# The edges of a fused two-layer decoder kernel: other orders for the first loads, the first rounds and the last ones

## The reference

```python
x = layernorm(x + L0_attn(x, Wq, Wk, Wv, Wo, lambdas, ln_w))   # differential attention, 16 heads of 2, 4 kv heads
x = layernorm(x + L0_xattn(x, k, fside, ctx, ctx, 8))          # a long convolution over the sequence, gated by ctx
x = layernorm(x + L0_ffn(x, gate_up, down, router_w))          # 8 experts, top 2, silu gate
x = layernorm(x + L1_attn(x, w_qkv, w_o))                      # causal attention, 16 heads of 32
x = layernorm(x + L1_xattn(x, mask, ctx, ctx, wq, wk, wv, wo)) # one head of 512: softmax((x wq)(ctx|x wk)^T) v, then wo
x = layernorm(x + L1_ffn(x, W_gate, W_qkv))                    # gate picks one head's k and v per token; attention with 16 query heads
return x

def L1_ffn(x, W_gate, W_qkv):
    gating = softmax(x @ W_gate.T); idx = argmax(gating)
    q, k, v = split(x @ W_qkv.T, 3)
    k_shared = k[head idx];  v_shared = v[head idx] * max(gating)
    return softmax(causal(q_h @ k_shared.T / sqrt(hd))) @ v_shared     # for every head h
```

## Time and profile before

| stretch of the span (us) | stage | PE busy (us) | PE idle (us) |
|---|---|---|---|
| 0 to 496 | front | 460.56 | 35.4 |
| 496 to 750 | long convolution | 252.92 | 1.1 |
| 750 to 880 | middle | 123.58 | 6.4 |
| 880 to 1199 | experts | 316.95 | 2.1 |
| 1199 to 1360 | tail: start, rounds 0 and 1 | 148.16 | 12.8 |
| 1360 to 2085 | tail: steady and first closing rounds | 715.07 | 9.9 |
| 2085 to 2162 | tail: closing rounds, last batch | 56.53 | 20.5 |

### The profile page before, as it was taken

The page is one execution under the profiler, slowest core; times in us unless marked ns, Lnnn a source line. Parts: engine busy times, 40 slices in busy tenths (PEclk is TensorE's granted clock), DMA queues, the critical chain, the costliest instruction groups (busy, mean ns, idle before and its releaser), DMA issues. The chain is left out here.

```text
span 2161.9 us, 29351 instructions
## 1 busy us (share of the span) xinstructions
PE 2073.8 (96%) x11935; PEld 1211.4 (56%) x11935; DVE 1191.6 (55%) x1827; ACT 515.7 (24%) x783; POOL 579.7 (27%) x542
## 2 busy tenths in 40 slices
PE   7899999989999999999999998999999999999996
PEld 5444444434444477565565655656666666666654
DVE  2566666667777754122222326366757575847466
ACT  1444444440000121110111122122222222222111
POOL 2122222227999600111110312112222212121112
PEclk9999999999999999999999999999999999999998
DMA  8950000105111046421121602101010101000000
GB/s 173 101 52 30 30 30 20 61 21 220 43 43 43 25 164 230 157 69 64 64 68 54 219 1 99 49 1 49 1 59 1 59 1 40 1 30 11 1 11 20
DMA packets 66178, 130.62 MB, mean 60 GB/s; under 512 B 6432, under 2 KB 19872, under 8 KB 66048
## 3 DMA queue, kind: packets, MB, share of 16 engines
q1 hardware_dynamic: 45392, 76.44, 13.8%
q10 hardware_dynamic: 14976, 33.69, 4.2%
q0 software_dynamic: 5680, 18.62, 2.9%
HBM read 97.40 MB, written 41.81 MB: 64 GB/s over the span
## 5 line engine op out<-in xcount | busy, mean ns | idle before, releaser
L1006 PE MATMUL conv_conv<-kv,toep 128*128 128x512 f32 x576 | 247.6, 592 | 0.1
L2578 DVE RECIPROCAL tail_inv<-tail_ring 128x256 f32<-128x256 f32 x60 | 105.4, 1756 | 178.2 <-PE tail_ring L1893 178.0
L1566 PE MATMUL moe_gu_ps<-gu,xT_tile 128*128 x608 | 192.4, 459 | 0.0
L1006 PEld LDWEIGHTS conv_conv<-kv,toep 128*128 128x128 f32 x576 | 109.4, 190 | 138.2 <-issue 129.6
L1040 POOL TENSOR_TENSOR kv<-vT,cT 128x512 f32<-128x512 f32 x128 | 147.2, 1175 | 16.6 <-PE conv_conv L1006 12.8
L2258 POOL TENSOR_TENSOR tail_rstd_x<-tail_rstd_x,const_minus_half 128x2 f32<-128x2 f32 x31 | 21.7, 701 | 477.0 <-DVE tail_rstd_x L2529 477.0
L1566 PEld LDWEIGHTS moe_gu_ps<-gu,xT_tile 128*128 128x128 f32 x608 | 112.3, 190 | 66.5 <-issue 17.8
L2266 POOL TENSOR_SCALAR_AFFINE_SELECT tail_expT<-tail_expT 128x1024 f32<-128x1024 f32 x63 | 70.0, 1112 | 245.2 <-ACT tail_expT L2350 244.7
L574 POOL TENSOR_SCALAR_AFFINE_SELECT front_expT<-front_expT 128x2048 f32<-128x2048 f32 x32 | 64.2, 2007 | 213.5 <-ACT front_expT L630 213.5
L1648 DVE TENSOR_TENSOR moe_hid<-moe_gu_ps,moe_silu 128x352 f32<-128x352 f32 x39 | 20.5, 524 | 171.1 <-PE moe_gu_ps L1566 171.1
L1547 POOL DMA_INDIRECT xg<-x_after,tokens x37 | 35.0, 946 | 282.0 <-PE moe_xT_ps L1561 254.9
(11 more groups left out here) (409 smaller groups left out, 4010.5 us busy)
## 6 DMA issues: line engine op xcount, KB each, us to landing
toep<-toeplitz SPq DMA_DIRECT2D x32, 320.0 KB, 2.9
y_slots<-moe_y ACTq DMA_DIRECT2D x39, 256.0 KB, 2.0
gu<-in_L_ffn_gate_up_proj SPq DMA_DIRECT2D x5, 1408.0 KB, 12.7
toeplitz<-filt_rows SPq DMA_DIRECT2D x1, 6144.0 KB, 66.9
front_e<-in_ctx SPq DMA_DIRECT2D x8, 512.0 KB, 5.7
toeplitz<-filt_rows SPq DMA_DIRECT2D x2, 2048.0 KB, 89.5
x_after<-x SPq DMA_DIRECT2D x8, 512.0 KB, 4.9
tail_x<-x_after SPq DMA_DIRECT2D x8, 512.0 KB, 3.7
```

The costliest lines, as they stand in the source:

```text
L1006: ins = pe.matmul(bank, toep[p][:, mat * P:(mat + 1) * P], kv[p][:, c].rearrange("p b j i -> p (b j i)"), start=n == 0, stop=n == len(PART ...
L1566: ins = pe.matmul(gu_ps[:, s % 2, h, 0:HID], (xT if s else mid.xT_first)[:, c, :], wgu[c][:, e, h * HID:(h + 1) * HID], start=c == 0, stop ...
L2578: link.after(dve.reciprocal(inv[c % 2][:], bank[:, S:2 * S]))
```

## The change

It moves instructions and drops one PSUM view; no product is added or removed. In the order of the program:

- Front, loads: SP issues x of batch 0, wv, wk, wq, then the filter and the rest; wq goes through SP's queue and no longer through ACT's. PE waits for wv and wk apart, and for the first constant alone before the first transposes. ACT regroups its half of wq before it drains the first values.
- Front, round 1 (a = 0): the first two `weigh` stand ahead of `scoreT` 2 and 4 (`soon`), as they already do for the last batch. The transposes of batch 3 move from the head of round 3 to behind `scoreT(1, 0)` of round 2.
- Front, last batch: DVE's `combine(7, 0, 1)` goes ahead of the second residual and the statistics of batch 6.
- Middle: PE's first pieces in another order.
- Tail start: the second half of the last `ctx_queries` goes behind the first `turn`, and the projections, scores and the second `turn` of batch 0 are interleaved anew.
- Tail round 1: `cross_turn(0, 1)` ahead of `weigh(P, 1, 1)` on PE; on DVE the norm of batch 2 and `mix(P, 1, 3)` earlier.
- Closing rounds: `maxima(A, h, 1)` ahead of `add_shared(a)`; `pick("v", c, 1)` behind `add_shared(h)`.
- Last batch: `ring_s` and the fourth exponential buffer go; of the four transposed score products only the second uses the ring's banks, the fourth comes after two `weigh`.

```diff
-        pe.wait_ge(constants_made, 7)
+        pe.wait_ge(constants_made, 1)
         for r, d, a, f, u in rounds():
-            if d is not None and d != 2: turn_input(d)
+            if d is not None and d not in (2, 3): turn_input(d)
             if d == 0:
+                pe.wait_ge(constants_made, 7)
                 xT_taken(d)
-                pe.wait_ge(weights_loaded, 32)
+                pe.wait_ge(weights_loaded["wv"], 16)
                 value(d)
+                pe.wait_ge(weights_loaded["wk"], 16)
                 key(d)
...
                 scoreT(a, 0)
-                if a == 0: turn_input(2)
+                if a < 2: turn_input(a + 2)
                 if u is not None: octets(u)
...
                     pe.wait_ge(wo_loaded, 64)
-                if f is not None and a < B - 1: out(f, 0)
-                if a == B - 1: weigh(a, 0, 0)
+                soon = a in (0, B - 1)
+                if f is not None and not soon: out(f, 0)
+                if soon: weigh(a, 0, 0)
                 scoreT(a, 2)
                 if a == B - 1: out(f, 0)
-                else: weigh(a, 0, 0)
+                if not soon: weigh(a, 0, 0)
                 scoreT(a, 3)
-                if f is not None and a < B - 1: out(f, 1)
-                if a == B - 1: weigh(a, 0, 1)
+                if f is not None and not soon: out(f, 1)
+                if soon: weigh(a, 0, 1)
                 scoreT(a, 4)
                 if a == B - 1: out(f, 1)
-                else: weigh(a, 0, 1)
+                if not soon: weigh(a, 0, 1)
                 scoreT(a, 5)
...
         load_x(0)
+        for k in ("wv", "wk"):
+            sp.dma_start(wide[k][:], w[k].rearrange("(c p) e -> p c e", p=P)).then_inc(weights_loaded[k], 16)
+        sp.dma_start(wq_rows, w["wq"].rearrange("(c p) e -> p c e", p=P)).then_inc(wq_loaded, 16)
         sp.dma_start(filt, filters).then_inc(filt_loaded, 16)
-        sp.dma_start(wide["wk"][:], w["wk"].rearrange("(c p) e -> p c e", p=P)).then_inc(weights_loaded, 16)
-        sp.dma_start(wide["wv"][:], w["wv"].rearrange("(c p) e -> p c e", p=P)).then_inc(weights_loaded, 16)
         load_x(1)
...
     def _(act):
-        act.dma_start(wq_rows, w["wq"].rearrange("(c p) e -> p c e", p=P)).then_inc(wq_loaded, 16)
         wo_rows = w["wo"].rearrange("(g k d) e -> g d k e", g=4, d=32)
...
             take(("turn", 0, n), pair(xT, n))
+        act.wait_ge(wq_loaded, 16)
+        act.copy(by_group(wide["wq"][:], "p c (j k d) -> p c j k d")[:, :, 2:4],
+                 by_group(wq_rows, "p c (k j d) -> p c j k d")[:, :, 2:4]).then_inc(wq_grouped, 1)
         take_value(0)
...
         take_key(0)
-        act.wait_ge(wq_loaded, 16)
-        act.copy(by_group(wide["wq"][:], "p c (j k d) -> p c j k d")[:, :, 2:4],
-                 by_group(wq_rows, "p c (k j d) -> p c j k d")[:, :, 2:4]).then_inc(wq_grouped, 1)
         act.wait_ge(lam_exp_in, 1)
...
         for r, d, a, f, u in rounds():
-            if d is not None and d not in (0, 2):
+            if d is not None and d not in (0, 2, 3):
                 for n in range(2):
...
                 exps(a, 0)
-                if a == 0:
+                if a < 2:
                     for n in range(2):
-                        take(("turn", 2, n), pair(xT, n))
+                        take(("turn", a + 2, n), pair(xT, n))
                 exps(a, 1)
...
             if a is not None: combine(a, 0, 0)
+            if a == B - 1: combine(a, 0, 1)
             if f is not None:
...
                 statistics(f)
-            if a is not None: combine(a, 0, 1)
+            if a is not None and a < B - 1: combine(a, 0, 1)
             if f is not None: norm(f)
...
-    return quads_r if (kind, b) == ("A", B - 1) and c % 2 else quads
-
-def ring_of(kind, b):
-    return ring_s if (kind, b) == ("A", B - 1) else ring
+    return quads_r if (kind, b, c) == ("A", B - 1, 1) else quads
...
 def exp_buf(kind, b, c):
-    if (kind, b, c) == ("A", B - 1, 3):
-        return wide["wk"][:].rearrange("p c (n q) -> p c n q", q=P)
     return expT[used.setdefault((kind, b, c), len(used)) % 3]
...
-        ctx_queries(B - 2)
+        for j in range(2):
+            ctx_queries(B - 2, j)
         for t in range(NT):
             ctx_values(B - 2, t)
-        ctx_queries(B - 1)
+        ctx_queries(B - 1, 0)
...
         turn("P", "x3", 0)
+        ctx_queries(B - 1, 1)
         pe.wait_ge(loaded["wq"], 16)
...
         cols("P", "k", 0, 0, wide["wk"])
+        cols("P", "q", 0, 1, wide["wq"])
         score("P", 0, 0)
-        cols("P", "q", 0, 1, wide["wq"])
+        cols("P", "k", 0, 1, wide["wk"])
         score("P", 0, 1)
-        cols("P", "k", 0, 1, wide["wk"])
-        score("P", 0, 2)
         pe.wait_ge(loaded["wv"], 16)
         rows("P", "v", 0, 0, xT[0], wide["wv"])
+        score("P", 0, 2)
+        turn("P", "x3", 1)
+        rows("P", "v", 0, 1, xT[0], wide["wv"])
         score("P", 0, 3)
-        rows("P", "v", 0, 1, xT[0], wide["wv"])
-        turn("P", "x3", 1)
         turned("P", 1)
...
         scoreT("P", 1, 2)
+        cross_turn(0, 1)
         weigh("P", 1, 1)
-        cross_turn(0, 1)
         scoreT("P", 1, 3)
...
         scoreT("A", c, 2)
+        pe.wait_ge(quads_r.drained_sem(("A", "T", c, 1)), quads_r.count(("A", "T", c, 1)))
+        weigh("A", c, 0)
+        weigh("A", c, 1)
         scoreT("A", c, 3)
-        pe.wait_ge(quads.drained_sem(("A", "T", c, 2)), quads.count(("A", "T", c, 2)))
-        for k in range(NC):
-            weigh("A", c, k)
-        banks = [ring_s.claim(pe, ("A", "o", c, t)) for t in range(NT)]
+        weigh("A", c, 2)
+        weigh("A", c, 3)
+        banks = [ring.claim(pe, ("A", "o", c, t)) for t in range(NT)]
         for k in range(NC):
             if k < NC - 1:
-                key = ("A", "W", c, k)
-                pe.wait_ge(ring_s.drained_sem(key), ring_s.count(key))
+                drained(("A", "W", c, k))
             for t in range(NT):
...
                 if k == NC - 1:
-                    ins.then_inc(ring_s.filled_sem(("A", "o", c, t)), 1)
+                    ins.then_inc(ring.filled_sem(("A", "o", c, t)), 1)
...
         norm("x5", c)
+        maxima("A", h, 1)
         add_shared(a)
-        maxima("A", h, 1)
         maxima("A", h, 2)
...
         maxima("A", c, 1)
-        pick("v", c, 1)
         maxima("A", c, 2)
...
         add_shared(h)
+        pick("v", c, 1)
         statistics("x6", h)
...
             mix("A", c, n)
-        bank = filled(("A", "W", c, 3), ring_s)
...
```

59 lines of the change are left out of this document (30 added, 29 removed).

## The result

The changed kernel took 2148.53 us in the median of six runs (2145.67 to 2154.64); the one before, beside it, 2167.70 (2163.63 to 2175.84). The medians lie 19.2 us apart. The ratio of the two kernels is 0.9915 with a 95% interval of [0.9897, 0.9933], which makes 18.4 us less, between 14.5 and 22.3. The forecast was 2145, range 2137 to 2158, and 19.2 us less from profile to profile. The two profiled executions differ by 18.0: the span fell from 2161.9 to 2143.9 us.

A forecast was written before the change was run, and what follows sets the result against it. TensorE, busy 96%, bounds the kernel, so only its 88 us of idle time and low-clock stretches can give. Terms sum to 19.2: 2163.7 - 19.2 = 2144.5, plus half a microsecond, 2145; range 2137 to 2158.

The forecast's parts named there:

- First loads: Start of the front: x alone arrives sooner, so the first query starts earlier; gain 4.2 us, from 2.8 to 4.8.
- Front, round 1: `weigh` ahead of `scoreT` fills idle time but delays ScalarE's third and fifth scores; -0.3 us, from -2.0 to +0.5.
- Front, last batch: Second half of `combine` done before TensorE asks, the sums' copy late next; gain 0.8 us, from 0.5 to 1.1.
- Middle: Start of the middle: wait of 2.2 us and low-clock stretch of 1.66 go; gain 3.8 us, at least 2.2.
- Tail, start: Four waits on ScalarE's drains, 3.9 us, get other products in between; gain 3.6 us, from 3.0 to 3.9.
- Tail, round 1: Waits for mask, norm and last `mix` shrink, 2.6 of clock returns; gain 5.3 us, from 2.1 to 5.7.
- Closing rounds and last batch: Earlier maxima, +0.7 us (0.3 to 0.9); first `mix` earlier, set by VectorE's norm, +1.0 (-1.0 to +1.5).
- the 10 below which I would have called myself wrong: Whole kernel: sign of a wrong forecast, the sum of TensorE's idle time falling by less than 10 us.
- (1): Rival: waits go but the clock is not given back, there or elsewhere; gain 14.9, 2148.8 us; chance 0.20.
- (2): Rival: waits are swapped, not removed (both rounds 1, closing rounds, last batch); gain 7.9, 2155.8 us; chance 0.20.
- (3): Rival: slower, shifted work brings new low clock stretches, 1.7 to 2.6 us each; 2175 with twelve; chance 0.04.
- (4): Rival at the first loads: x is no earlier; 1.4 less, 2146 us; included in the forecast's 0.56.

The follow-up runs named there:

- the ninth experiment: The kernel before with the new order of the tail's round 1 alone; 2165.06 us, one execution.
- The second experiment: The changed kernel with the front's round 1 in the old order and combine(7,1,0)'s first products ahead of batch 6's norm; 2144.60 us, ratio to before 0.9897.
- the sixth experiment: The kernel before with the middle stage's new order alone; 2163.90 us, ratio to before 0.9974.

## Why the prediction was right, and where it was wrong

*First loads, 4.2 forecast, 3.86 measured: right.* x came alone, and wq on the same queue no longer held it up. wq itself was at hand at 10.76, later than the 8 to 9 that I had taken from the transfer rate, but regrouped 1.5 us before the query needed both halves; that margin, not my figure, carried the step. The other traces with these loads gave 2.8 to 4.2, so 4.2 is at their upper end.

*Front, round 1, -0.3 forecast within -2.0 to +0.5, -3.2 measured: wrong in size.* The mechanism was named: `scoreT` 2 and 4, the third and the fifth, stand behind a `weigh` that waits for its mask, and ScalarE, which sets this round's pace, gets its scores late. I had priced it at 0.35 each. The order's own price is read best from the exps, first start to last, over all traces: with the new order 20.1 to 21.2 us in six traces, with the old one 18.9 to 19.1 in five and 20.8 in two whose round 1 ran longest at the lower clock. So it is about 1.2, inside the bounds; the failed step is the price of 0.35 each. The third scores came no later (2.10 of idle time ahead of their exp, 2.45 in the old order); nearly all of it is the fifth, 3.84 against 1.39. The other 2 us of the 3.2 go with the clock, 0.80 against 0.90 in the mean. Whether the order brings that is not settled: from 51 to 140 us the six traces with the new order changed their lead by +0.4 to -3.2, 2.0 lost in the mean, the seven with the old one (the kernel before is the zero among them) by +1.7 to -4.9, 1.0 lost. The sixth and the ninth experiment, whose front is the old one word for word, lost 4.6 and 4.9 there, more than the changed kernel; a loss of 3.2 is thus no proof of the order. For this step no bound of mine allowed for the clock, though the kernel before had two low stretches in this very round.

*Front, last batch, 0.8 forecast, 0.0 measured: wrong.* I had seen that TensorE asks for `combine(7, 0, 1)` too early, and named the sums' copy as what is late next. It was VectorE itself: the same residual, statistics and norm stand ahead of `combine(7, 1, 0)` in either order, so two waits became one of the same sum. The second experiment moved the norm too and got 1.09.

*Middle, 3.8 forecast, 4.23 measured: right*, both parts: the wait of 2.20, and 8.80 - 7.07 = 1.73 of clock; of the 0.3 more I put 0.17 down to overlap. That the clock goes with the gap is shown by the counts: with a gap there (2.20 or 2.63 us) the stretch was low in four traces of five, without one in none of eight. The fifth, the one with the first loads alone, says that the 1.73 is not there to be gained every time. By the Trainium skill, "TensorE: Matmul & The Clock Gate", section "PE-mode transpose", which the prediction weighed, 2.2 was to be expected. Ahead of `ctx_queries` stand 32 transposes with no other work in the stage, and the clock stayed at 1.00 behind them, in the changed kernel and in the sixth experiment, at two times of the span. In this kernel the trace decides against it.

*Tail, start, 3.6 forecast, 4.69 measured: right, a little low.* I had taken off 0.3 for waits that might stay, and had not counted the overlap, if that is what the rest is.

*Tail, round 1, 5.3 forecast, 5.07 measured: right*, with 1.70 and not 1.4 of idle time left. The 2.6 of clock in it was partly luck: in two of the nine traces with this order the product took 8.80 behind 1.80 us of idle time, and the step gave 1.8, under my low end of 2.1. *Closing rounds and last batch, 1.7 forecast, 1.48 measured: right in size.* In the last batch the path was another than I had said: not VectorE's norm but `weigh` set the first `mix`, 0.3 behind the norm's end, because POOL took the norm's root ahead of the first mask; I had it the other way round, the root waiting for a mask. The fourth `weigh` was ready 0.07 us before it was needed, not 1.

What no term held is the 1.69 us of the tail's first product, which ran partly at the lower clock before and not after, with no edit near it. It made up half of round 1's loss, and the kernel with the first loads alone, whose tail product had full clock too, shows that it comes and goes by itself (eight of thirteen traces have it). With it the terms sum to 18.0; that my 19.2 came close is in part luck: a loss that I had sized too small and a gain that I hadn't foreseen stood against each other. The mechanism of most of the sum, idle time at the edges that the steady stages carry through, was right: the lead changed by only 0.04 between 1372 and 2075 us, and TensorE's idle time fell by 14.3 us, over the 10 below which I would have called myself wrong.

Of the rivals, (1) was wrong at both of its places in the changed kernel's trace, and right at the tail's in the two others named above. (2) was right at the front's last batch and in round 1, and nowhere else. (3) was wrong for the whole and right for a part: the front's round 1 ran longer at the lower clock. (4) was wrong.

## What to carry to other kernels

Where one engine is busy 96% of the time, look for the idle time at the seams, and price a wait at its bracket plus what the clock loses behind it, the second as a gain that comes in most executions and not in all. Before putting an instruction ahead of another to fill a wait, ask what the instruction itself waits for, and who waits for the one that it now holds up. A wait that an earlier result should remove stays if the engine that makes it does the same sum of work before the next thing that is asked of it: move the longest piece, not the nearest.

## What the runs showed of the hardware

How often a stretch at 1.2 GHz stood at the end of a wait of TensorE or right behind it, by place, over the thirteen traces:

| place | idle time (us) | the product behind it, when low (us) | low in |
|---|---|---|---|
| tail, round 1, old order | 2.9 | 8.80 to 9.82, not 7.1 | 4 of 4 |
| middle, wait there or put back | 2.2 to 2.6 | 8.61 to 10.23, not 7.07 | 4 of 5 |
| front, last batch, one wait | 2.7 | 5.18 and 5.37, not 3.67 | 2 of 5 |
| tail, start of the stage | 1.92 | 8.83, not 7.14 | 5 of 13 |
| tail, round 1, new order | 1.7 to 1.9 | 8.80, not 7.1 | 2 of 9 |
| middle, no wait | 0 | 7.07 | 0 of 8 |

At the same place the longer wait had a low stretch at it more often: 4 of 4 against 2 of 9 in the tail's round 1, 4 of 5 against none of 8 in the middle. But no length decided it: 2.7 us left the clock alone three times, and 1.80 us had a low stretch behind it twice. Where there was one, the product lost 1.5 to 3.2 us. What decides in the single case is open.

TensorE stood still for 1.1 to 4.5 us in the front near 147 us in seven of thirteen traces, at the same transposes and with no wait in the program; in four of them one record is missing just behind. What it is stays open. Together with the low stretches it makes up most of the 7.5 us between the two traces of the changed kernel. The leads of the middle's start and the tail's start repeat to 0.1 us meanwhile, and so a kernel should be judged here by the stage's lead as much as by its time; but those of the first loads and of both rounds 1 do not repeat, and want more than one trace.
